# An attention and feed-forward layer: who adds the relative bias, when z is made, and a last batch written out by hand

## What is computed

```python
def attn(x):                       # 16 heads of 8 dimensions
    q, k, v = split(x @ W_qkv + b_qkv)
    scores = einsum('bihd,bjhd->bhij', q, k) / sqrt(8)
    scores += rel_bias[clip(i - j + 128, 0, 256)]      # one table column per head
    return einsum('bhij,bjhd->bihd', softmax(scores), v) @ W_out + b_out

def ffn(x):                        # ternary weights times a scale for each output
    h = silu(lin1(x)) * lin2(x)    # 128 -> 512
    h = gelu(lin_h1(h)); h = gelu(lin_h2(h))           # 512 -> 512, twice
    return lin3(h)                 # 512 -> 128

x = x + layernorm(attn(layernorm(x)))
return x + layernorm(ffn(layernorm(x)))
```

## Time and profile before

| | before |
|---|---|
| median of the runs | 290.55 us (290.06 to 291.17) |
| the profiled execution | 290.61 us, span 288.8 us |
| mean granted clock of TensorE | 0.992 of full speed |
| TensorE busy | 267.7 us (93%), 1875 matmuls |
| VectorE busy | 212.5 us (74%), 442 instructions |
| ScalarE busy | 205.2 us (71%), 316 instructions |
| GpSimd busy | 102.5 us (35%) |
| chain that ended last | TensorE 68%, VectorE 16%, ScalarE 8%, issue 5% |

### The profile page before, as it was taken

How to read it: one execution, slowest core, us unless ns; L and a number is a source line. 1 busy time by engine, 2 the same in 40 slices (tenths; PEclk the granted TensorE clock), 3 DMA queues, 4 the chain that set the end, 5 groups by cost and what they waited for, 6 DMA issues and landing times.

```text
span 288.8 us, 5174 instructions
## 1 busy us (share of the span) xinstructions
PE 267.7 (93%) x1875; PEld 180.7 (63%) x1875; DVE 212.5 (74%) x442; ACT 205.2 (71%) x316; POOL 102.5 (35%) x107
## 2 busy tenths in 40 slices
PE   7899989899999999999999998999999999999980
PEld 7656646555555555556555554557888888888860
DVE  4576977889789789789788888857654853673675
ACT  2677777785876776785886886767459976896750
POOL 6716000101702603923974985117640202400111
PEclk9999999999999999999999999999999999999996
DMA  6979505322221262560221200000000000010012
GB/s 159 339 231 142 184 5 183 129 65 90 64 84 41 74 194 103 179 210 21 75 78 36 78 0 3 1 3 1 0 2 0 0 0 2 0 36 2 2 36 77
DMA packets 21356, 21.17 MB, mean 73 GB/s; under 512 B 3664, under 2 KB 18768, under 8 KB 21072
## 3 DMA queue, kind: packets, MB, share of 16 engines
q1 hardware_dynamic: 20464, 20.53, 24.4%
q10 hardware_dynamic: 864, 0.27, 0.4%
HBM read 14.90 MB, written 5.64 MB: 71 GB/s over the span
## 4 chain that ended last, share of the span: by engine, by line
PE 68%; DVE 16%; ACT 8%; issue 5%; DMA 1%; POOL 1%; ACTq 0%; POOLq 0%; DVEq 0%
PE place L1449 11%; PE place L1450 11%; PE place L1252 10%; PE pv L1304 7%; DVE mx L692 6%; PE place L1244 5%; ACT ring L1016 4%; PE place L1278 4%; DVE place L699 3%; PE place L1203 2%; PE misc L1315 2%; PE place L1289 2%; PE misc L1182 2%; PE pv L1450 2%; PE pv L1449 2%
## 5 line engine op out<-in xcount | busy, mean ns | idle before, releaser
L692 DVE TENSOR_REDUCE mx<-place 128x4 f32<-128x1024 f32 x64 | 78.3, 1223 | 16.2 <-PE place L1252 14.9
L517 POOL TENSOR_TENSOR rstd<-mv,mhalf 128x2 f32<-128x2 f32 (+1 forms) x26 | 20.9, 806 | 145.8 <-DVE mv L624 145.8
L1016 ACT ACTIVATE ring<-place 128x1024 f32<-128x1024 f32 x64 | 65.7, 1028 | 6.4 <-PE place L1289 3.1
L1252 PE MATMUL place<-room,identr 128*128 128x512 f32 x128 | 47.0, 448 | 0.0
L1023 ACT COPY place<-raw 128x1024 f32<-128x1024 f32 x37 | 37.8, 1024 | 11.7 <-DVE mx L692 11.7
L1449 PE MATMUL place<-room,w_hi 128*128 128x512 f32 (+1 forms) x116 | 44.7, 387 | 0.7 <-DVE room L825 0.7
L1450 PE MATMUL place<-room,w_hi 128*128 128x512 f32 (+1 forms) x116 | 44.1, 383 | 0.0
L1304 PE MATMUL pv<-ring,vx 128*9 128x256 f32 x512 | 33.6, 380 | 0.4 <-ACT ring L1016 0.4
L825 DVE TENSOR_TENSOR room<-ring,room 128x512 fp32r<-128x512 f32 x32 | 21.3, 690 | 17.1 <-ACT room L1104 17.1
L1244 PE MATMUL place<-room 33*128 33x256 f32 x256 | 28.4, 298 | 4.9 <-ACT ring L1016 4.8
L1278 PE MATMUL place<-room 33*128 33x256 f32 x256 | 31.7, 328 | 1.4 <-DVE place L699 1.1
(11 more groups left out here) (141 smaller groups left out, 434.4 us busy)
## 6 DMA issues: line engine op xcount, KB each, us to landing
raw<-ext SPq DMA_DIRECT2D x8, 384.0 KB, 6.8
room<-q_parts SPq DMA_DIRECT2D x48, 64.0 KB
room<-k_parts SPq DMA_DIRECT2D x48, 64.0 KB
w_lo<-h SPq DMA_DIRECT2D x2, 1024.0 KB, 5.6
q_parts<-w_hi SPq DMA_DIRECT2D x4, 256.0 KB, 3.0
k_parts<-w_hi SPq DMA_DIRECT2D x2, 512.0 KB, 3.4
xs<-x SPq DMA_DIRECT2D x3, 256.0 KB, 6.1
w_lo<-w SPq DMA_DIRECT2D x3, 256.0 KB, 2.8
```

What stands on the lines that cost most here:

```text
L517: nc.gpsimd.tensor_tensor(rstd[:, at:at + width], mv[:, at:at + width, 1], mhalf[:, 0:width], ALU.pow).then_inc(rstd_set, 1)
L692: nc.vector.tensor_reduce(mx[:, s // RPAIRS, :, :, s % RPAIRS].rearrange("p i k -> p k i"), max_tile(b * PAIRS + s)[:, :, :].rearrange("p ...
L1016: nc.scalar.activation(probs[:, s % PRING, :, :, :].rearrange("p k j n -> p (k j n)"), score_tile(b * PAIRS + s)[:, :, :].rearrange("p k n ...
L1252: last = mm(max_tile(b * PAIRS + s)[:, half, :], identr[:, :], windows(table_hi[:, 2 * s + half, :], 0, P, 2, S), start=False, stop=True, ...
```

## The change

- `BY_PE` becomes empty: in batches 0 to 6 no bias is added by TensorE. `BY_DVE` becomes (1, 2, 5), so ScalarE has 0, 3, 4, 6 and 7. Bias 1 of the next batch is written by VectorE in slot 7 behind the maximum; bias 1 of batch 0 ahead of the loop.
- In the last batch TensorE adds the bias in slots 3 and 6, VectorE writes 1, 2, 4, 5 and 7, ScalarE 0.
- z has two places for even and odd batches. `norm_T`, `keep_zT` and `z_low` in slot 7 work on batch b-2 instead of b-1; in batch 6, both batch 4 (slot 6) and batch 5 (slot 7) are done.
- The last batch is taken out of the loops on all three engines and written out in an order of its own.
- Batch 5 has two matmuls on zeros in slot 6. `zeros` and `ones` become one tensor. GpSimd makes two low tables instead of one.

The core of the diff:

```diff
-BY_PE = (7,)
-BY_DVE = (2, 5)
-LAST_BY_DVE = (1, 2, 4, 5, 6)
+BY_PE = ()
+BY_DVE = (1, 2, 5)
+LAST_BY_PE = (3, 6)
+LAST_BY_DVE = (1, 2, 4, 5, 7)
+LOW_PAIRS = BY_PE + tuple(s for s in LAST_BY_PE if s not in BY_PE)
...
             def second_norm(b):
                 dve.wait_ge(rstd_set, b * 2 + NU + 2)
-                if b > 0:
-                    dve.wait_ge(zT_ready, b)
+                if b > 1:
+                    dve.wait_ge(zT_ready, b - 1)
...
-            for b in range(B):
+            for s in range(2):
+                if s in BY_DVE:
+                    dve.wait_ge(raw_in[s], 16)
+                    write_bias(s)
+            for b in range(B - 1):
                 for s in range(PAIRS):
...
+                        write_bias(b * PAIRS + s + 2)
+                    elif (s + 2) % PAIRS < 2 and (s + 2) % PAIRS in BY_DVE and b + 2 < B:
                         write_bias(b * PAIRS + s + 2)
...
-                        if s == 7 and b + 1 < B:
-                            z_low(b - 1)
+                            if b + 2 == B:
+                                z_low(b - 2)
+                        if s == 7:
+                            if b + 2 == B:
+                                write_bias((b + 1) * PAIRS + 1)
+                                z_low(b - 1)
+                            elif b > 1:
+                                z_low(b - 2)
+
+            first = (B - 1) * PAIRS
+            write_bias(first + 2)
+            weigh(B - 2, 0)
+            write_bias(first + 4)
+            write_bias(first + 5)
+            weigh(B - 2, 1)
+            write_bias(first + LAST_BY_DVE[-1])
+            largest_low()
+            attn_moments(B - 2)
+            any_low()
+            residual(B - 2)
+            second_norm(B - 2)
...
+            last = B - 1
+            probabilities(last, 0)
+            keep_weighted(last - 1, GROUPS - 1)
+            minus_max(last, 1)
+            probabilities(last, 1)
+            probabilities(last, 2)
+            keep_weighted(last, 0)
+            probabilities(last, 3)
+            probabilities(last, 4)
+            keep_weighted(last, 1)
+            keep_onT(last - 1)
+            probabilities(last, 5)
+            probabilities(last, 6)
+            keep_weighted(last, 2)
+            probabilities(last, 7)
...
+                        if b == 5:
+                            stream(misc, blank, blank, BLANKS[0])
+                        if b + 2 == B:
+                            norm_T(b - 2)
...
+            last_scores(0)
+            pe.wait_ge(z_lo_set, B - 2)
+            maxima_T(B - 1, 1)
+            weighted(B - 2, GROUPS - 1)
+            last_scores(1)
+            pe.wait_ge(mrow_set, B * RANGES)
+            back(B - 2, 0)
+            last_scores(2)
+            weighted(B - 1, 0)
+            last_scores(3)
+            back(B - 2, 1)
+            last_scores(4)
+            weighted(B - 1, 1)
+            heads_T(B - 2)
+            last_scores(5)
+            last_scores(6)
+            project(B - 2)
+            weighted(B - 1, 2)
+            last_scores(7)
+            pe.wait_ge(y_read, B - 1)
+            pe.wait_ge(w_low_top_set, 2)
+            mm(misc[0:1, 0:P], w_low_top[:, :], ident[:, :], start=True, stop=True).then_inc(w_low_row, 1)
+            weighted(B - 1, 3)
```

More of the change, by code:

```diff
@@ L164, in build @@
         y = y_and_z[:, 0:TPB * D].rearrange("p (t d) -> p t d", t=TPB)
-        z = y_and_z[:, TPB * D:2 * TPB * D].rearrange("p (t d) -> p t d", t=TPB)
+        z_odd = sb("z_odd", [P, TPB * D])
+        z_places = (y_and_z[:, TPB * D:2 * TPB * D], z_odd[:, :])
+        z = [z_places[b % 2].rearrange("p (t d) -> p t d", t=TPB) for b in range(B)]
         w_low_top = sb("w_low_top", [P, 1])
@@ L343, in by_dve, with by_pe @@
             return BY_DVE if b + 1 < B else LAST_BY_DVE
+        def by_pe(b):
+            return BY_PE if b + 1 < B else LAST_BY_PE
         def by_act(b):
-            return tuple(s for s in range(PAIRS) if s not in BY_PE + by_dve(b))
+            return tuple(s for s in range(PAIRS) if s not in by_pe(b) + by_dve(b))
         BLANKS = (2, 2, 2, 6, 6)
@@ L542, in _, with table_low @@
             table_high(7)
-            for i, s in enumerate(BY_PE):
+            def table_low(s):
+                i = LOW_PAIRS.index(s)
                 pool.wait_ge(table_hi_pool, s + 1)
@@ L547, in _ @@
                                         ALU.subtract).then_inc(table_lo_set, 1)
+            for s in LOW_PAIRS:
+                table_low(s)
             x_inv_std(4)
@@ L1038, in _ @@
             write_bias(0)
-            for b in range(B):
+            for b in range(B - 1):
                 for s in range(PAIRS):
                     ahead = b * PAIRS + s + 1
-                    if ahead < B * PAIRS and ahead % PAIRS in by_act(ahead // PAIRS):
+                    if ahead % PAIRS in by_act(ahead // PAIRS):
                         write_bias(ahead)
@@ L1063, in _ @@
                             keep_xT(4)
+                            for u in range(1, 3):
+                                act.wait_ge(parts_out[u], PARTS_OUT)
                         if b in (2, 3):
                             q_and_k_high(4, b - 2)
[L1066 to L1070, removed]
+                        if b + 2 == B:
+                            keep_zT(b - 2)
+                    if s == 7:
+                        if b + 2 == B:
+                            keep_zT(b - 1)
+                        elif b > 1:
+                            keep_zT(b - 2)
+            last = B - 1
[13 more added lines that the diff above has]
+            probabilities(last, 7)
             nc.scalar.activation(table_loaded[:, :], mhalf[:, 0:1], ACT.Silu)
@@ L1279, in scores @@
                                   rows(k_rows, b, half, s)[:, j * P:(j + 1) * P], rows(q_rows, b, half, s),
-                                  start=(s in BY_PE and j == 0), stop=False, skip_group_check=True)
-                if s not in BY_PE:
+                                  start=(s in by_pe(b) and j == 0), stop=False, skip_group_check=True)
+                if s not in by_pe(b):
                     last.then_inc(st_ready, 1)
             def score_bias(b, s):
-                if b == 0:
-                    pe.wait_ge(table_lo_set, BY_PE.index(s) + 1)
+                low = LOW_PAIRS.index(s)
+                pe.wait_ge(table_lo_set, low + 1)
                 for half in range(2):
-                    for part in (table_hi[:, 2 * s + half, :], table_lo[:, LOW_AT_SLOT[2 * s + half], :]):
+                    for part in (table_hi[:, 2 * s + half, :], table_lo[:, 2 * low + half, :]):
                         last = mm(score_tile(b * PAIRS + s)[:, half, :], identr[:, :], windows(part, 0, P, 2, S),
@@ L1360, in _ @@
             v(2)
-            for b in range(B):
-                more = b + 1 < B
+            for b in range(B - 1):
                 for s in range(PAIRS):
-                    if more or s not in BY_PE:
-                        scores(b, s)
-                    if s == 6 and 1 <= b <= 4:
+                    scores(b, s)
+                    if s == 6 and b > 0:
                         pe.wait_ge(mrow_set, b * RANGES + 3)
@@ L1376, in _ @@
                             v(4)
[L1377 to L1380, removed]
+                        if b == 5:
+                            stream(misc, blank, blank, BLANKS[0])
+                        if b + 2 == B:
+                            norm_T(b - 2)
+                    max_scores(b + 1, s)
+                    max_bias(b + 1, s)
+                    if s in BY_PE:
                         score_bias(b, s)
-                    if s + 1 in BY_PE and not more:
-                        scores(b, s + 1)
-                        score_bias(b, s + 1)
                     if s == 0:
@@ L1426, in _ @@
                             v(3)
-                    if s == 5 and more:
+                    if s == 5:
                         if b == 0:
@@ L1432, in _ @@
                         maxima_T(b + 1, 0)
[L1433 to L1436, removed]
+                    if s == 7 and b > 1:
+                        if b in (2, 3):
                             pe.wait_ge(qk_lo_set, 5 + b)
```

54 lines of the change are left out of this document (22 added, 32 removed).

## The result

| | before | after |
|---|---|---|
| median of the runs | 290.7 us (290.06 to 291.17) | 300.9 us (294.72, 297.64, 304.13, 305.53) |
| mean granted clock of the same runs | 0.992 (profiled) | 0.974, 0.959, 0.938, 0.926 |
| profiled execution | 290.6 us, span 288.8 | 305.5 us, span 303.6 |

The ratio is 1.019 (95% interval 1.014 to 1.024). By the medians it is 1.035. The forecast was 291.4 us, range 288.8 to 293.5: wrong. No run of the changed kernel lies in the range.

The account below looks back on a forecast made before the run. TensorE ends batches 1 to 4 late, VectorE batches 5 and 6. Terms +1.0 +0.7 -0.55 -0.31 -0.31 -0.68 +0 +1.0 = +0.85 us on 290.6 gave 291.4 us, range 288.8 to 293.5.

Parts of the forecast that it names:

- Bias 1 of batch 0 on VectorE: Start of batch 0: bias 1 ready at 35.93 us, scores of slot 2 at 38.4, loss 1.0 us.
- x normalization behind bias 1: End of batch 0: bias 1 stands ahead of the last x unit's normalization, maximum 1 at 58.96 us, loss 0.7.
- Gains in batches 1 to 4: Batch borders without bias matmuls: net gains 0.55, 0.31, 0.31 and 0.68 us, together 1.85.
- Batches 5 and 6 gain nothing: Borders of batches 5 and 6: the maximum of slot 6 on VectorE is late as before, gain 0.
- The last batch: Rebuilt last batch: slot-1 scores 1.2 us later behind the low z, last weighted matmuls at 193.9 us, loss 1.0.
- The rest of the span behind it: Feed-forward part after the last weighted matmuls: starts when these end and shifts with them, no added time.
- the wait of 2 us in the last batch: TensorE idle about 2.1 us (177.8 to 179.9) before the transposes of the maxima; not yet long enough to lower the clock.
- the rival of a falling clock: Last batch: matmuls at half speed behind the gap cost some 3 us, giving 294.5 us; chance 0.05.

Follow-up runs that it names:

- e4: Changed kernel, order kept, with matmuls on zeros in the two long waits (batch 0 and last batch): median 291.3 us, ratio 1.001, low clock in 4 of 12.
- e6: Changed kernel, nothing reordered, with matmuls on zeros in both long waits and at the batch borders: median 291.45 us, ratio 1.003, low clock in 0 of 11.
- e7: Kernel before the change with only bias 1 of batch 0 moved to VectorE: median 292.8 us, ratio 1.009, low clock in 2 of 4.
- e8: e5 with the last x unit's normalization moved from slot 7 of batch 0 to slot 2 of batch 1: median 288.6 us, ratio 0.994.
- e9: Changed kernel with matmuls on zeros at the batch borders only, long waits left empty: median 296.3 us, ratio 1.018, low clock in 6 of 6.
- e3: Changed kernel with bias 1 of batch 0 back on ScalarE and the last batch reordered: median 289.1 us, ratio 0.993, low clock in 3 of 8.
- e5: e3 with four matmuls on zeros added for each batch border: median 289.2 us, ratio 0.995, low clock in 0 of 6.
- e10: e3 with the old split of biases in batches 0 to 6, TensorE adding 3 and 7 in the last: median 291.3 us, ratio 1.002.
- e2: Changed kernel, last batch reordered: low z before bias 1, weighted(6, 3) before the transposes of the maxima. Median 295.6 us, ratio 1.009, low clock in 6 of 6.

## Why the prediction was wrong

**The sum of the schedule was right, in part by luck.** With the clock held and nothing reordered the changed schedule takes 291.0 us (median of the eight such executions of e4) to 291.45 (e6), up to 0.4 us of it the added matmuls on zeros; the forecast was 291.4. Two of its terms are off by about 0.5 us, in opposite directions, as the profile of e4 shows:

- Bias 1 of batch 0 on VectorE, +1.0: right (35.93 and 38.41 in the profile after; e7 without a fall +1.0).
- x normalization behind bias 1, +0.7: right (e8: 0.8).
- Gains in batches 1 to 4, 1.85: right in kind, 0.5 too small. Between the marks of batches 1 and 5 e4 takes 137.61 - 55.16 = 82.45 us, against 138.35 - 54.42 = 83.93 before. That is 1.5 less; the forecast's distances of marks for this piece, the x normalization counted in, add up to 82.9, 1.0 less.
- Batches 5 and 6 gain nothing: 157.78 - 137.61 = 20.17 after 19.97, the 0.34 us by which VectorE is late behind batch 4 being in it. Right.
- The last batch, +1.0: right in kind (the wait is 0.70 us plus the eight matmuls on zeros that fill its first part), a little smaller in size. In e4 the last `weighted` starts at 193.07, 35.3 us behind the mark of batch 6, where it was 34.6: +0.7.
- The rest of the span behind it grew by 0.6 us in e4 (96.5 to 95.9), which the forecast had at 0. What makes it is open. This and the gains that came out larger cancel.

**The step that failed is the clock.** The prediction named the wait of 2 us in the last batch, said the clock would stay, and gave the opposite 0.05. Its other wait, in batch 0, it priced at 1.0 us as if a microsecond of standing still cost only itself. Both can open a fall. In the profile after they are followed by 6.8 and 13.7 us at 1.2 GHz, and a fall costs about half the stretch in which TensorE is the one waited for: 4 to 5 us for the last one (e9 against e6), against the 1.2 us for which the forecast had the wait. So the rival of a falling clock had the right mechanism, at the wrong price: 3 us for one fall, where the profiled execution has four, 37.6 us at 1.2 GHz before the final one, and is 14 us over the forecast.

The trace of before showed waits of up to 0.77 us with a granted clock of 1.00 beside them, and I read that as room to spare. It only said that this much idle time, with this much work around it, had not been too much. The Trainium skill (TensorE: Matmul & The Clock Gate, "Why this matters for your kernels") warns of idle gaps longer than those of this kernel, and I took shorter ones for safe. The measured waits, 0.92 and 1.84 us, are shorter, and the clock fell behind them. Here the measurement decides: the rule is no licence for shorter gaps.

**The second cause I had counted as harmless.** In batches 5 and 6 the removed matmuls buy no time, so the same stretch holds 0.95 us less work of TensorE, and a wait of 0.65 us stands in its place. I had written that as "gain 0". It wasn't 0: e3 falls in batches where no wait of even 0.8 us stands, and e5 and e10 don't fall. Whether the missing work or the pair of waits that it leaves is what counts, these runs don't separate: the matmuls on zeros fill both. That the matmuls on zeros act through the clock and not through the order is shown by e4 against the changed kernel, and by e5 against e3: their order of real work is the same, and so within 0.4 us is the time wherever the clock held (289.2 and 288.8 us).

Theory A (long waits alone) fell with e3, theory B (thin borders alone) with e9. Theory C, both together, predicted e5, e6 and e10. The first cause is shown on one chip (e7 against the kernel before beside it: 2 of 4 against 0 of 17) and in the profiles. The second rests on executions on different chips and on the places of the falls in the traces, and is likely rather than shown. What stays open: why executions of one kernel differ (e3 between 288.5 and 301.1 us), that is, what decides whether a given wait is followed by a fall in this execution.

## What to carry to other kernels

When a change takes matmuls away but another engine ends the stretch, TensorE's work in that stretch becomes thinner without the time falling. Price the clock then, not only the order: every new wait of TensorE of about a microsecond, and every new pair of shorter ones close together, is a possible fall, worth several microseconds in the dense part behind it. A few matmuls on zeros in the waits tell at once whether it is the clock, and cost little (0.4 us in e5 against the executions of e3 in which the clock held). Look at the granted clock of several executions before believing a median.

## What was not expected of the hardware

- A wait of 0.92 us in front of otherwise dense matmuls was followed by 1.2 GHz in the profile after and by a lower mean clock in 2 of 4 executions of e7. The same wait (0.90 to 0.92 us) passed at full clock in the profiles of e2, e7 and e9.
- The lower level can last far longer than the wait: 13.3 us (57.6 to 70.9) with TensorE's row full all the time, though only 3.4 us in the short ones of e2 and e3. Dense matmuls did not bring the upper level back at once.
- A busy share of 92 to 93% with the clock at 0.93 and at 0.99 alike: the share can't show the loss. The sixteen matmuls of `weighted` at 1.05 and 1.90 us can.
